# Two layers of a decoder written as one turn, and a mixture layer that multiplies by resident weights

## The reference, cut to what matters

```python
def _L2_attn_ref(x, proj_w, proj_b, filter_time):          # long convolution, ORDER = 2
    p = (x @ proj_w + proj_b).reshape(B, L, order + 1, D)
    v = p[:, :, 0, :]
    for stage in range(order):
        conv = irfft(rfft(v, n=fft_size) * rfft(filter_time[stage], n=fft_size))[:, :L, :]
        v = conv * p[:, :, stage + 1, :]
    return v

def _L2_xattn_ref(query, value, ...):                      # random-feature attention, one head
    Q, K, V = query @ Wq + bq, value @ Wk + bk, value @ Wv + bv
    Q_hat = cos(Q @ random_weights + random_bias)
    K_hat = cos(K @ random_weights + random_bias)
    return softmax(Q_hat @ K_hat.T) @ V

def _L2_ffn_ref(x, ...):                                   # mixture, E = 15 experts, top 3
    shared = relu(xt @ sW1 + sb1) @ sW2 + sb2
    top_p, top_i = top_k(softmax(xt @ router_W + router_b), 3)
    # each token adds p * (relu(x @ eW1[e] + eb1[e]) @ eW2[e] + eb2[e]) for its three experts e
```

## Time and profile before

| | |
|---|---|
| median of 3 runs | 2776.63 us (2773.84 to 2779.97) |
| the profiled execution's own time | 2774.84 us |
| its span, first to last instruction | 2773.1 us |
| mean granted clock of TensorE | 0.907 |
| busy: PE, DVE, ACT, GpSimd | 2315.0, 1422.1, 1025.0, 699.1 us |
| moved by DMA | 143.66 MB |

### The profile page before, as it was taken

One profiled execution on the slowest core, in us unless ns is written; L12 is line 12 of the kernel. 1 busy time (PEld: TensorE's weight loads), 2 busy tenths in 40 slices (PEclk: granted clock), 3 DMA queues, 4 the chain that ended last, 5 costly groups with the idle time before them and its releaser, 6 DMA issues. The chain is left out here.

```text
span 2773.1 us, 39253 instructions
## 1 busy us (share of the span) xinstructions
PE 2315.0 (83%) x13092; PEld 1663.2 (60%) x13092; DVE 1422.1 (51%) x4229; ACT 1025.0 (37%) x2591; POOL 699.1 (25%) x656
## 2 busy tenths in 40 slices
PE   7985499878869839985788789698899798899898
PEld 5763377655547518864367566465466576466576
DVE  3555022256758765547123467544677443677454
ACT  3433111145525510035022156343565432565432
POOL 1102311110024343211633200263443100433111
PEclk9987699979969859997799899899999999999899
DMA  9032211173000010030287411400000000000000
GB/s 245 1 151 81 83 50 42 46 150 13 1 6 1 5 53 1 1 126 1 92 240 209 145 36 25 152 11 31 1 1 1 1 1 1 1 1 1 20 23 20
DMA packets 121173, 143.66 MB, mean 52 GB/s; under 512 B 47507, under 2 KB 101013, under 8 KB 119184
## 3 DMA queue, kind: packets, MB, share of 16 engines
q1 hardware_dynamic: 112240, 120.16, 15.5%
q0 software_dynamic: 8736, 20.99, 2.1%
HBM read 96.18 MB, written 47.90 MB: 52 GB/s over the span
## 5 line engine op out<-in xcount | busy, mean ns | idle before, releaser
L249 PE MATMUL bank<-work,weights 128*128 128x256 f32 (+3 forms) x2432 | 541.3, 380 | 42.2 <-DMA work<-in_weights 21.1
L249 PEld LDWEIGHTS bank<-work,weights 128*128 128x128 f32 (+1 forms) x2432 | 415.5, 193 | 138.2 <-DMA work<-in_weights 27.8
L249 PE MATMUL bank<-weights,work 128*128 128x256 f32 (+4 forms) x1520 | 412.6, 409 | 53.1 <-POOL work L2318 35.0
L249 PEld LDWEIGHTS bank<-weights,work 128*128 128x128 f32 (+1 forms) x1520 | 278.5, 196 | 152.7 <-issue 68.3
L633 POOL TENSOR_TENSOR work<-work,minus_half 128x2 f32<-128x2 f32 x96 | 69.7, 726 | 859.0 <-DVE work L626 859.0
L249 PE MATMUL bank<-weights,x_feat 128*128 128x512 f32 (+2 forms) x576 | 211.5, 500 | 25.5 <-PEq L211 14.6
L658 ACT COPY x_feat<-bank 128x512 f32<-128x512 f32 x80 | 46.7, 584 | 343.3 <-PE bank L650 342.9
L249 PEld LDWEIGHTS bank<-weights,x_feat 128*128 128x128 f32 x576 | 106.1, 196 | 84.2 <-issue 60.1
L249 PE MATMUL bank<-x_feat,weights 128*128 128x256 f32 (+3 forms) x400 | 120.4, 479 | 35.6 <-PEq L211 31.0
L4090 ACT ACTIVATE work<-work 128x128 f32<-128x128 f32 (+1 forms) x256 | 137.0, 543 | 1.5 <-DVE work L4162 1.5
L1523 DVE TENSOR_TENSOR work<-bank,work 128x384 f32<-128x384 f32 (+1 forms) x64 | 31.4, 491 | 189.6 <-ACT work L1441 189.6
(11 more groups left out here) (461 smaller groups left out, 4651.3 us busy)
## 6 DMA issues: line engine op xcount, KB each, us to landing
weights<-in_weights SPq DMA_DIRECT2D x62, 256.0 KB
weights<-in_weights SPq DMA_DIRECT2D x1, 12296.0 KB
weights<-in_weights SPq DMA_DIRECT2D x1, 9360.0 KB
weights<-in_weights SPq DMA_DIRECT2D x1, 8488.0 KB
work<-rows_in SPq DMA_DIRECT2D x62, 129.0 KB
rows_in<-ident SPq DMA_DIRECT2D x2, 3968.0 KB, 36.7
weights<-rows_back SPq DMA_DIRECT2D x8, 768.0 KB, 4.5
work<-rows_in SPq DMA_DIRECT2D x8, 645.0 KB, 4.2
```

The source lines that it names most:

```text
L249: ins = nc.tensor.matmul(out, lhsT, rhs, start=(i == 0), stop=(i == len(pairs) - 1))
```

## The change

The two layers of the convolution and the attention become one turn. `long_convolution` and `random_feature_attention` now return five generators (one per engine) which yield at the end of each step; `run_stages` runs the first layer's generator and, from its step t = 7, one yield of the second layer's behind each. The attention's fold is its first yield. Its semaphores are others of the same turn (`later_signals`). The convolution's filters, products and sums move from the scratch to the words above its weights; the load of layer 8's weights waits for the convolution's last residual.

In the mixture all of `w1` stays in SBUF: two sheets lie above the weights, the slots and their loads are gone, only the bias is loaded per tile. The rows are now the stationary operand and the expert's 256 columns the moving one, addressed by register; so the product comes out by row, is copied by ACT (`store_mid`), turned by PE (`turn_mid`, banks 6 and 7) and then gets bias and relu. The second layer follows one step later.

```diff
+def later_signals(S):
+    N = Names()
+    N.aux_done = S.mid_turned
...
+def run_stages(nc, K, first, second, start):
+    signals = K.S
+    def program_of(a, b, engine):
+        later = b(engine)
+        for t, _ in enumerate(a(engine)):
+            if t >= start:
+                K.S = K.S_next
+                next(later, None)
+                K.S = signals
+        K.S = K.S_next
+        for _ in later:
+            pass
+        K.S = signals
+    with turn(nc, K) as block:
+        @block.tensor
+        def _(pe):
+            program_of(first.tensor, second.tensor, pe)
...
@@ one_head: project @@
+        if not keys:
+            ready(pe, b)
@@ long_convolution @@
-    filt = A(ORDER, 2, 3 * D)
-    part = A(2, 2, 2 * D)
-    spec = A(2, 4, D)
+    above = K.weights[:, words(6):words(6) + 7 * 1024]
+    filt = above[:, 0:3 * 1024].rearrange("p (s f d) -> p s f d", s=ORDER, f=2)
...
@@ random_feature_attention @@
+    c = one_head(nc, K, A, W, scored, lambda pe, b: pe.wait_ge(earlier.xT_stored, b + 1))
+    def sync(sp):
+        sp.wait_ge(earlier.residual_done, B)
+        follow_weights(sp, K, 7)
+        yield
+    def tensor(pe):
+        weights_are_in(pe, K, 7)
+        pe.wait_ge(earlier.q_stored, 3 * B)
...
-                    if b:
-                        pe.wait_ge(S.probs_done, b)
+                if b:
+                    pe.wait_ge(S.probs_done, b)
+                else:
+                    pe.wait_ge(earlier.probs_done, 4 * B)
                 c.scores(pe, b)
...
+def convolution_and_features(nc, K):
+    earlier = K.S
+    first = long_convolution(nc, K)
+    K.S_next = later_signals(earlier)
+    K.S = K.S_next
+    second = random_feature_attention(nc, K, first, earlier)
+    K.S = earlier
+    run_stages(nc, K, first, second, 7)
@@ mixture_top3 @@
-    sheets = [K.weights[:, 0:TILES * ROW], K.weights[:, above:above + TILES * ROW],
+    sheets = [K.weights[:, above:above + TILES * ROW], K.weights[:, above + TILES * ROW:above + 2 * TILES * ROW],
+    mid = hid[:, 0, :].rearrange("p (n d) -> p n d", n=2)
...
-                    sp.dma_start(slots_w[j % SETS], parts[:, bass.ds(e, 1), :].rearrange("p e (k c) -> p (e k) c", k=KT)
-                                 ).then_inc(K.expert_loaded[j % SETS], 16)
...
-            def hidden(j):
-                pe.wait_ge(K.expert_loaded[j % SETS], 32 * (j // SETS + 1))
+            def inner(j, e):
                 pe.wait_ge(S.row_stored, j + 1)
+                if j >= 2:
+                    pe.wait_ge(S.mid_stored, j - 1)
+                mm(nc, K.bank[2 + j % 2][:, 0:D],
+                   [(xT[:, j % 2, k, :], W["w1"][:, bass.ds(2 * e + k, 1), :].rearrange("p o c -> p (o c)"))
+                    for k in range(KT)]).then_inc(S.inner_done, 1)
+            def turn_mid(j):
+                pe.wait_ge(S.mid_stored, j + 1)
                 if j >= 2:
                     pe.wait_ge(S.inner_stored, j - 1)
                 for m in range(2):
+                    ins = nc.tensor.transpose(K.bank[6 + j % 2][:, m * P:(m + 1) * P], mid[:, j % 2, m * P:(m + 1) * P],
+                                              K.ident[:])
+                ins.then_inc(S.mid_turned, 1)
...
+            for t in range(TILED + 3):
+                if t < TILED:
+                    turn_row(t)
+                if t % REGS == 1 and t <= TILED:
+                    n = min(REGS, TILED - (t - 1))
+                    at = (t - 1) // REGS % 2 * REGS
+                    pe.reg_load(owners[at:at + n], table[0:1, t - 1:t - 1 + n])
...
+                if 1 <= t <= TILED:
+                    inner(t - 1, of[t - 1])
+                if 2 <= t <= TILED + 1:
+                    turn_mid(t - 2)
+                if 3 <= t:
+                    outer(t - 3, of[t - 3])
...
+            def store_mid(j):
+                a.wait_ge(S.inner_done, j + 1)
+                if j >= 2:
+                    a.wait_ge(S.mid_turned, j - 1)
+                nc.scalar.copy(mid[:, j % 2, :], K.bank[2 + j % 2][:, 0:D]).then_inc(S.mid_stored, 1)
+            def rectify(j):
+                a.wait_ge(S.mid_turned, j + 1)
+                a.wait_ge(K.expert_loaded[j % SETS], 16 * (j // SETS + 1))
...
+            for t in range(1, TILED + 2):
+                if t <= TILED:
+                    store_mid(t - 1)
+                if t >= 2:
+                    rectify(t - 2)
...
-                if j >= 2:
-                    store_out(j - 2)
+                if t >= 3:
+                    store_out(t - 3)
```

More of the change, by code:

```diff
@@ new lines, in sync, with gpsimd, combine @@
+    def sync(sp):
+        follow_weights(sp, K, 6)
+        yield
+    def gpsimd(p):
+        def combine(q):
+            for f in range(2):
+                p.wait_ge(S.probs_done, 2 * q + f + 1)
+                if q >= 2:
+                    p.wait_ge(S.out_done, q - 1)
+                for which, op in ((0, ALU.subtract), (1, ALU.add)):
+                    ins = nc.gpsimd.tensor_tensor(spec[:, q % 2, f + 2 * which, :], part[:, f, which, 0:D],
+                                                  part[:, f, which, D:2 * D], op)
+                ins.then_inc(S.pool_step, 1)
+        for t in range(STEPS):
+            if (b := at_step(t, 1, B)) is not None:
+                combine(2 * b)
+            if (b := at_step(t - 1, 1, B)) is not None:
+                batch_power(nc, p, K, tail, b)
+            if (b := at_step(t, 1, B)) is not None:
+                combine(2 * b + 1)
+            yield
@@ new lines, in scalar @@
+    def scalar(a):
+        for s in range(ORDER):
+            a.wait_ge(S.aux_done, s + 1)
+            for f in range(2):
+                bank = K.bank[3 + 2 * s + f]
+                nc.scalar.copy(filt[:, s, f, 0:2 * D], bank[:, :])
+                ins = nc.scalar.copy(filt[:, s, f, 2 * D:3 * D], bank[:, 0:D])
+            ins.then_inc(S.aux_stored, 1)
+        for t in range(STEPS):
+            if (b := at_step(t - 2, 1, B)) is not None:
+                batch_store(nc.scalar.copy, a, K, b, X)
+            yield
@@ L2605, with random_feature_attention @@
+    program = Names()
+    program.sync, program.gpsimd, program.tensor, program.scalar, program.vector = sync, gpsimd, tensor, scalar, vector
+    program.end = A.at
+    return program
 TWO_PI = 2 * np.pi
 ROUND = 1.5 * 2 ** 23
-def random_feature_attention(nc, K):
-    W, S, A = weights_of(K, 7), K.S, Arena(K)
+def random_feature_attention(nc, K, first, earlier):
+    W, S, A = weights_of(K, 7), K.S, Arena(K, first.end)
     quarter, biases = A(1), A(2, KT)
@@ new lines, in tensor @@
+        pe.wait_ge(S.hid_stored, 3)
+        yield
+        for t in range(STEPS):
+            if (b := at_step(t, 1, B)) is not None:
+                if b:
+                    pe.wait_ge(S.q_turned, 2 * b)
+                c.project(pe, folded[:, 1, :, :], b, True)
+            if (b := at_step(t, 1, B)) is not None:
+                if b:
+                    pe.wait_ge(S.q_turned, 2 * b - 1)
+                c.project(pe, folded[:, 0, :, :], b, False)
+            if (b := at_step(t - 1, 1, B)) is not None:
+                if b:
+                    pe.wait_ge(S.probs_done, b)
+                else:
+                    pe.wait_ge(earlier.probs_done, 4 * B)
+                c.scores(pe, b)
+            if (b := at_step(t - 2, 1, B)) is not None:
+                c.turn_probs(pe, b)
+            if (b := at_step(t, 1, B)) is not None:
+                c.values(pe, b)
+            if (b := at_step(t - 2, 1, B)) is not None:
+                c.products(pe, b)
+            if (b := at_step(t - 4, 1, B)) is not None:
+                if b == 0:
+                    pe.wait_ge(earlier.y_added, B)
+                c.turn_x(pe, b)
+            yield
```

605 lines of the change are left out of this document (292 added, 313 removed).

## The result

The changed kernel takes **2734.8 us** (median of 4 runs, 2730.1 to 2741.2), the kernel before beside it 2775.2 (4 runs): ratio 0.9856, 95% interval 0.9833 to 0.988. In a second comparison of 5 and 11 runs it was 2734.7 against 2775.8, ratio 0.9847 (0.9834 to 0.986). The forecast was 2744, its range began at 2737: faster, as said, but by 9.2 us more than the number and 2.2 us more than the range allowed.

The account below looks back on a forecast made before the run. PE was taken to bound the tile loop and ACT the attention, with waits at the seam. 2774.84 less 14.8 (seam) and 18.4 (loop) is 2741.6; from the median 2743.4, said as 2744 us, range 2737 to 2763.

Parts of the forecast that it names:

- The seam: Between convolution and attention: the fold fills PE's wait, first cosine at 1212.6 us against 1227.43, 14.8 us earlier.
- ACT carries this to the attention's end: In the attention: ACT sets a 6.80 us period, so the end comes 14.8 us earlier, like the start.
- The loop: Mixture's tile loop: PE needs 2.19 us a tile; end at 1529.4 instead of 1547.83 us, 18.4 us earlier.
- 3 us for all (bounds: nothing, and 4 x 3.8): In the tile loop: cost of layer 9's four 960.5 KB weight chunks, 2.6 us each, 1.9 spare.
- slack in the ring: Mixture's row buffers: a round of 15.6 us for 8 tiles against PE's 17.5, with 1.9 us to spare.
- The 59 steps: In the tile loop: from the fourth step at 1393.2 us, 59 steps of 2.19 us to 1522.4.
- The base: Whole kernel: gains taken from one profiled execution of 2774.84 us, 1.8 us below the median of three runs.
- The range's low end: Whole kernel: 2737 us, granting 1 us to the seam, 3 to no stall in the loop, 3 to run spread.
- Rival (a): Tile loop: the ring of row buffers sets the pace, 2.64 us a tile; kernel 2762 us, halfway 2753; chance 0.17.
- Rival (b): Between convolution and attention: the seam gives little, down to 5 us; kernel 2753 us; chance 0.12.
- Rival (c): Tile loop: transposes lower PE's clock; with half the loop at 1.2 GHz, kernel 2805 us; chance 0.06.
- The rule that was weighed: Tile loop's transposes: the skill's 275 ns each, not counting for the clock, would add 0.33 us a tile, kernel 2762.

Follow-up runs that it names:

- e3: The changed kernel with the second layer started at step 12 instead of 7, so the attention's fold stands behind all convolution steps: 2749.7 us, ratio 0.9902.
- e12: The changed kernel with the second layer started at step 6 instead of 7: 2731.6 us, ratio 0.9844.
- e1: The kernel before with only the new mixture, convolution and attention still as two turns: 2755.5 us, ratio 0.9918.
- e2: The changed kernel with the old mixture, so only convolution and attention are merged: 2758.9 us, ratio 0.9943.
- e7: The changed kernel with the two transposes of each tile's middle issued twice: 2747.4 us, ratio 0.9901.
- e8: The changed kernel with first-layer weights stationary again, in slots ACT fills from the resident copy, without transposes of the middle: 2724.0 us, ratio 0.981.
- e11: The changed kernel with layer 9's four weight chunks issued behind the loads of the rows back, not in the loop: 2737.1 us, ratio 0.986.
- e15: The changed kernel with seven row buffers instead of eight: 2749.4 us.

## Why the prediction was right and wrong, point by point

**The seam** was right in its places: the first projection at 1205.9 us (forecast 1205.9), the first cosine at 1212.6 (1212.6), the fold under the inverse transform's wait, the layer's load hidden. The turn gained 15.4 us against 14.8 (15.1 in the second profile). That the places agree to 0.1 us is in part luck: they are counted from the last forward transform, and in the turn's own time the first cosine gained 13.9 and 14.7 us; the prediction's own terms (1205.5 + 5.64 + 1.28) put it 0.2 us earlier than it wrote. The rest came behind it: of the three periods that are shorter than 6.8 us, in before as well, the first went from 6.14 to 5.75 us, and in the first profile the stretch behind the last cosine was 1.1 us shorter. So "ACT carries this to the attention's end" held to within 1.5 us. e3 shows the cause: the order of the steps is worth 14.3 us, the barrier 0.9. e12 shows that what remains is no single delay: with the copy of the last batch out of the first cosine's way, PE's last inverse transform holds it. That the parts come out additive (e1, e2) was assumed and holds.

**The loop** was right in kind: PE sets a tile, 2.17 us for a forecast 2.19 (e7, e8). The term that failed is "3 us for all (bounds: nothing, and 4 x 3.8)" for the chunks: they cost nothing (e11: 138.9 us without them, 138.3 and 138.9 with them). Its 3.8 us is a wait beside a 256 KB load, and those loads go. The prediction's slack in the ring, 1.9 us, was less than the 2.6 us of a chunk and yet each was taken up; with one buffer fewer they seem no longer to be (e15). The 59 steps came 1.0 us shorter (2.173 us each), the drain 0.1 to 0.3 longer: 132.4 us from the fourth step to the end, where 136.2 were said. The loop gained 22.1 us, and since 0.8 us were lost ahead of it and behind it, the mixture's turn 21.3 in the first two profiles, not 18.4.

**The base** was the other step that failed, and no term of the sum shows it. The sum was made against one execution and moved to the median by 1.8 us, as if its parts were typical too. They weren't: its mixture's turn was 306.6 us where four profiles have a mean of 309.5, and the turns ahead of it were at the long end. The old loop's waits and its clock vary from run to run, and a change that removes the stalls gains their mean, not their size in the one profile at hand.

The 9.2 us between forecast and result can be counted so: 2.9 from the mixture's turn (21.3 for 18.4), 0.6 from the seam, 2.9 from the base (309.5 for 306.6, four profiles, so no sharp figure), 2.0 from the rest of the base (1.4 from a median of 2776.6 that is 2775.2 with a fourth run, 0.6 from rounding up). That leaves 0.8, well inside the spread of the runs. The range's low end had granted 1 us to the seam, 3 to the chunks and 3 to the runs: right for the terms, with nothing for a loop whose length before wasn't known to 3 us.

**Rival (a)**, the ring sets the pace: wrong at eight buffers, right at seven and fewer. The sign named for it, "PE or SyncE waiting for rows or landings", was half wrong: SyncE waited 42.6 us and PE not at all. **Rival (b)**, the seam gives little: wrong. **Rival (c)**, the clock of the loop: wrong, 1.00 in the steady part with two, four and six transposes in a tile.

**The rule that was weighed.** In e7 two more transposes cost 0.22 us a tile and the clock stays at the higher of its two levels (2.4 GHz) with transposes in 27% of PE's time. The Trainium skill (TensorE: Matmul & The Clock Gate, Part 4: PE-mode transpose) gives about 275 ns for one in a kernel, which its single record here shows too (272 to 273 ns of duration), but in the stream each one more costs 0.11 us. Its statement that transposes don't engage the clock doesn't show in this loop; no run here has a stretch of transposes alone. The prediction's estimate from the page's figure was 2762 us; its own 0.33 us a tile are 20 us, which from 2743.4 gives 2764.

## What to carry to other kernels

When a change removes a stall, read that stall in more than one profiled execution, or widen the range by what it varies: here 306.6 to 313.3 us for one turn of the same kernel. Price a ring as a law, not as a number: stages that the bounding engine issues in order lengthen with the tile, so n buffers allow fixed time / (n - stages). Close to PE's own pace that law was too kind (seven buffers), and a single large load may then cost what it doesn't cost with one buffer more. When a term is priced from a wait in the kernel before, ask what stood beside that wait, and whether the change takes it away. And where resident weights bring transposes with them, ask which engine is idle: a copy of 0.62 us on ACT was cheaper than 0.2 us of transposes on the engine that sets the pace.

## What the runs showed of the hardware that was not expected

- The same turn, with the same waits and far from any edit, took 165.6, 169.6 or 172.7 us, in groups within 0.3 us of each other, with granted clocks of 0.97 to 0.93; the groups do not follow the kernel, and the end of the turns ahead moved by 7 us (1027.4 to 1034.5).
- With the 256 KB loads kept and only ACT's bias wait behind them, a loop of 138.3 us took 157.4 at a DMA share of 0.79; without the loads, moving the chunks out (a share of 0.44 for 0.61 between 1400 and 1440 us) changed nothing.
- The four longest waits of PE in the loop before (12.6 of 21.1 us) ended 6 to 8 us behind the four 960.5 KB chunks; beside no 256 KB loads the same chunks cost nothing with eight buffers.
- With seven buffers a tile took 2.42 us, where PE's work is 2.17 and the ring's law allows 2.31.
